# A block's 256 columns split into even and odd dims instead of two sets of samples, with an addition on VectorE before the sums over dims

## The reference

```
h = x
for i in 0, 1, 2:                       # W_i: (200, H_i * 40), H = 40, 100, 100
    p[b, h*40+m, d] = h[b, h, d] * x[b, m, d]
    y = relu(einsum('oi,bid->bod', W_i, p) + bias_i)
    h, direct_i = first and last 100 of y   # the last layer: all 200 are direct
z = concat(direct_0, direct_1, direct_2).sum over d      # (512, 400)
out = relu(relu([z, dense] @ W_top1 + b) @ W_top2 + b) @ W_top3
```

## Time and profile before

| | |
|---|---|
| median of 3 runs | 2904.6 us (2903.6 to 2905.39) |
| profiled execution | 2907.22 us, its span 2905.5 us |
| TensorE, matmuls busy | 2830.5 us, 97% of the span |
| VectorE busy | 2607.7 us, 90% |
| ScalarE busy | 1502.0 us, 52% |
| GpSimd busy | 688.1 us, 24% |

### The profile page before, as it was taken

How to read it: one execution, slowest core, us unless ns; L and a number is a source line. 1 busy time by engine, 2 the same in 40 slices (tenths; PEclk the granted TensorE clock), 3 DMA queues, 4 the chain that set the end, 5 groups by cost and what they waited for, 6 DMA issues and landing times.

```text
span 2905.5 us, 54782 instructions
## 1 busy us (share of the span) xinstructions
PE 2830.5 (97%) x19516; PEld 2811.0 (97%) x19516; DVE 2607.7 (90%) x1751; ACT 1502.0 (52%) x1880; POOL 688.1 (24%) x669
## 2 busy tenths in 40 slices
PE   2899999999999999999999999999999999999998
PEld 2899999999999999999999999999999999999996
DVE  4899999999999999999999999999999999999993
ACT  2555555555555555555555555555555555555552
POOL 2122222222222222222222222222222222222000
PEclk8999999999999999999999999999999999999999
DMA  6434333334333334333334334334333334334320
GB/s 158 101 67 100 86 74 97 86 74 98 87 74 96 87 74 99 87 74 97 87 75 98 86 74 97 87 75 96 89 73 96 88 75 99 87 75 94 95 57 21
DMA packets 280089, 249.92 MB, mean 86 GB/s; under 512 B 27803, under 2 KB 278602, under 8 KB 279965
## 3 DMA queue, kind: packets, MB, share of 16 engines
q1 hardware_dynamic: 211192, 196.57, 23.8%
q0 software_dynamic: 59744, 45.90, 11.0%
q10 hardware_dynamic: 9129, 7.13, 1.0%
HBM read 140.44 MB, written 4.20 MB: 50 GB/s over the span
## 4 chain that ended last, share of the span: by engine, by line
PE 96%; DMA 1%; SPq 1%; DVE 1%; issue 1%; ACT 0%; POOL 0%; DVEq 0%; ACTq 0%; POOLq 0%
PE acc L717 62%; PE acc L719 29%; PE z_ps L734 3%; PE hid_ps L730 1%; SPq L349 1%; PE acc L777 0%; DMA x_pairs<-x_rows 0%; DVE product L660 0%; DMA raw_weights<-in_w 0%; DVE tails L665 0%; PE hid_ps L800 0%; SPq L321 0%; DMA hid_rep<-hid 0%; POOL gathered L410 0%; DMA starts_sb<-in_table_starts 0%
## 5 line engine op out<-in xcount | busy, mean ns | idle before, releaser
L717 PE MATMUL acc<-weights,heads 126*128 126x400 f32 (+1 forms) x9088 | 2707.9, 365 | 62.3 <-DVE tails L665 62.3
L719 PE MATMUL acc<-weights,tails 126*128 126x200 f32 (+1 forms) x9088 | 2324.3, 256 | 0.0
L484 ACT ACTIVATE heads<-product 126x1024 fp32r<-126x1024 f32 (+2 forms) x1152 | 1203.9, 1048 | 1149.9 <-PE acc L719 749.5
L717 PEld LDWEIGHTS acc<-weights,heads 126*128 126x128 f32 (+1 forms) x9088 | 1717.0, 189 | 63.8 <-issue 46.6
L719 PEld LDWEIGHTS acc<-weights,tails 126*128 126x128 f32 (+1 forms) x9088 | 1744.7, 192 | 0.0
L660 DVE TENSOR_TENSOR product<-hid_rep,x_rep 126x2048 f32<-126x2048 f32 x512 | 1172.5, 2290 | 214.8 <-PE acc L719 175.5
L665 DVE TENSOR_TENSOR tails<-product,heads 126x1024 fp32r<-126x1024 f32 (+2 forms) x1152 | 1338.4, 1203 | 3.4 <-ACT heads L484 3.4
L418 POOL TENSOR_TENSOR wait_taker<-wait_taker 1x1 f32<-1x1 f32 x192 | 106.8, 556 | 2069.0 <-ACT acc_copy L490 2067.3
L410 POOL DMA_INDIRECT gathered<-in_table,rows_now x150 | 316.5, 2110 | 45.7 <-issue 45.7
L495 ACT ACTIVATE y_relu<-acc_copy 128x400 f32<-128x400 f32 x192 | 102.4, 533 | 192.8 <-DMA acc_copy<-acc_copy 192.8
L419 POOL DMA_DIRECT2D acc_copy<-acc_copy x192 | 175.8, 916 | 1.1 <-issue 0.6
(11 more groups left out here) (27 smaller groups left out, 106.4 us busy)
## 6 DMA issues: line engine op xcount, KB each, us to landing
x_rep<-x_rows SPq DMA_DIRECT2D x512, 120.0 KB
hid_rep<-hid SPq DMA_DIRECT2D x512, 120.0 KB
x_pairs<-x_rows SPq DMA_DIRECT2D x192, 280.0 KB
acc_copy<-acc_copy POOLq DMA_DIRECT2D x192, 200.0 KB
hid_rep<-hid SPq DMA_DIRECT2D x512, 5.0 KB
x_pairs<-x_rows SPq DMA_DIRECT2D x64, 120.0 KB
raw_weights<-in_w ACTq DMA_DIRECT2D x12, 492.2 KB
x_rep<-x_rows SPq DMA_DIRECT2D x128, 20.0 KB
```

What stands on the lines that cost most here:

```text
L484: act.activation(heads[0:rows, ring % HEADS_RING, 0:tiles, :], product[0:rows, ring % PRODUCT_RING, 0:tiles, :], ACT.Copy).then_inc(heads_ ...
L717: nc.tensor.matmul(acc[:, at.parity, c, 0:2 * LAYER], heads[0:rows, ring % HEADS_RING, k, cols], w, start=(q == 0 and k == 0), stop=False)
L719: last = nc.tensor.matmul(acc[:, at.parity, c, LAYER:2 * LAYER], tails[0:rows, ring % PRODUCT_RING, k, cols], w[:, 0:LAYER], start=False, ...
```

## The change

- `c` now means the parity of the dim, not the half of the samples: `dims(columns, c)` is `columns[:, c:256:2]`. The stationary operands of L717 and L719 are read with a step of two, and the transposes write `hid_ps` with a step of two, so that it has the columns in the old order. Row r of both result halves belongs to sample r // 16.
- VectorE gets a new instruction, `fold`: it adds the two halves of the direct outputs of `y_relu` into `y_fold`, 100 elements a partition for layers 0 and 1, 200 for layer 2. It waits for `y_relued` and for the turn before (`y_turned`).
- `turn` sums `y_fold` with `sum16` (128 x 8), one matmul for each 100 outputs in place of two, and waits for `y_folded` between the transposes and the sums.
- VectorE's order in the steady state: the fold of the step before's layer 2 lies between the tails of groups 2 and 3 of layer 1, the fold of layer 0 behind the tails of groups 4 and 5 of layer 1, the fold of layer 1 between the tails of groups 4 and 5 of layer 2.

```diff
+DIM_HALF = DIM // CG
...
+        y_fold = sb("y_fold", [128, LAYER])
...
-        sum32 = sb("sum32", [128, 128 // DIM])
+        sum16 = sb("sum16", [128, BLOCK])
...
+        def dims(columns, c):
+            return columns[:, c:COLS:CG]
...
+            def fold(layer, at, b):
+                first = HALF if layer < 2 else 0
+                dve.wait_ge(y_relued, at.slot + 1)
+                above_zero(dve, y_turned, at.slot)
+                dve.tensor_tensor(y_fold[:, first:LAYER], y_relu[:, 0, first:LAYER], y_relu[:, 1, first:LAYER],
+                                  ALU.add).then_inc(y_folded, 1)
+
-            def make_previous_tails(g, ring):
+            def make_previous_tails(g, ring, between=None):
                 layer, q = previous[0]
-                for n in (2, 1):
-                    make_tails(layer, q + 2 - n, g - n, (ring - n) % RING)
+                make_tails(layer, q, g - 2, (ring - 2) % RING)
+                if between:
+                    fold(*between)
+                make_tails(layer, q + 1, g - 1, (ring - 1) % RING)
                 previous[0] = None
...
+                        between = None
+                        if first and layer == first[0] and q == 4 and before and before[0] > 0:
+                            between = before
+                        if second and layer == second[0] and q == 6:
+                            between = first
                         if previous[0]:
-                            make_previous_tails(at.group + q, at.ring + q)
+                            make_previous_tails(at.group + q, at.ring + q, between)
+                            if l0 and first and layer == first[0] and q == 6:
+                                fold(*l0)
...
-                        cols = slice(c * 128, (c + 1) * 128)
-                        nc.tensor.matmul(acc[:, at.parity, c, 0:2 * LAYER], heads[0:rows, ring % HEADS_RING, k, cols], w,
+                        nc.tensor.matmul(acc[:, at.parity, c, 0:2 * LAYER], dims(heads[0:rows, ring % HEADS_RING, k, :], c), w,
                                          start=(q == 0 and k == 0), stop=False)
-                        last = nc.tensor.matmul(acc[:, at.parity, c, LAYER:2 * LAYER], tails[0:rows, ring % PRODUCT_RING, k, cols],
+                        last = nc.tensor.matmul(acc[:, at.parity, c, LAYER:2 * LAYER], dims(tails[0:rows, ring % PRODUCT_RING, k, :], c),
                                                 w[:, 0:LAYER], start=False, stop=(q == last_q and k == tiles - 1))
...
-                        nc.tensor.transpose(hid_ps[0:HALF, layer, c * 128:(c + 1) * 128], y_relu[:, c, 0:HALF], ident[:, :])
+                        nc.tensor.transpose(dims(hid_ps[0:HALF, layer, 0:COLS], c), y_relu[:, c, 0:HALF],
+                                            ident[:, :])
+                pe.wait_ge(y_folded, at.slot + 1)
                 for n, first in enumerate((HALF,) if layer < 2 else (0, HALF)):
-                    for c in range(CG):
-                        at_col = n * BLOCK + c * (BLOCK // CG)
-                        last = nc.tensor.matmul(z_ps[0:HALF, at.parity, at_col:at_col + BLOCK // CG],
-                                                y_relu[:, c, first:first + HALF], sum32[:, :], start=True, stop=True)
+                    last = nc.tensor.matmul(z_ps[0:HALF, at.parity, n * BLOCK:(n + 1) * BLOCK],
+                                            y_fold[:, first:first + HALF], sum16[:, :], start=True, stop=True)
```

More of the change, by code:

```diff
@@ L76, in cin_kernel @@
 def cin_kernel(nc, ids, table_starts, table, w0a, w0b, w1, w2, dense_t, wt1z, wt1d, wt2, wt3, bt1, bt2,
-               ident_in, sum32_in, out):
+               ident_in, sum16_in, out):
     duos = ids.shape[1]
@@ L190, in cin_kernel @@
         y_relued = sem("y_relued")
+        y_folded = sem("y_folded")
         y_turned = sem("y_turned")
@@ L312, in _ @@
                 sp.dma_start(swapped(n), w0b[:, t:t + k, :]).then_inc(swapped_loaded[n], 16)
-            for dst, src in ((ident[:, :], ident_in), (sum32[:, :], sum32_in), (dense_sb[:, :], dense_t),
+            for dst, src in ((ident[:, :], ident_in), (sum16[:, :], sum16_in), (dense_sb[:, :], dense_t),
                              (wt1d_sb[:, :], wt1d), (wt3_sb[:, :], wt3), (bt1_sb[:, :], bt1), (bt2_sb[:, :], bt2)):
@@ L670, in _ @@
             previous = [None]
-            def make_previous_tails(g, ring):
+            def fold(layer, at, b):
[5 more added lines that the diff above has]
+            def make_previous_tails(g, ring, between=None):
                 layer, q = previous[0]
-                for n in (2, 1):
-                    make_tails(layer, q + 2 - n, g - n, (ring - n) % RING)
+                make_tails(layer, q, g - 2, (ring - 2) % RING)
+                if between:
+                    fold(*between)
+                make_tails(layer, q + 1, g - 1, (ring - 1) % RING)
                 previous[0] = None
             def step(i, odd):
+                before, l0, l1, l2 = slots_of(i, odd)
+                first, second = (l1, l2) if l1 else (l2, None)
                 for layer in range(3):
@@ L692, in step @@
                             make_previous_tails(at.group + 2, at.ring + 2)
+                        if before and before[0] == 0 and layer == 0:
+                            fold(*before)
                         if odd is None:
@@ L698, in _ @@
             make_previous_tails(total_groups, total_groups)
+            fold(2, place(2, blocks - 1), blocks - 1)
         @block.tensor
@@ L845, in lay_out @@
     packed["ident"] = np.eye(128, dtype=np.float32)
-    packed["sum32"] = np.repeat(np.eye(128 // DIM, dtype=np.float32), DIM, axis=0)
+    packed["sum16"] = np.repeat(np.eye(BLOCK, dtype=np.float32), DIM_HALF, axis=0)
     tables = [arr(f"tbl_{f}") for f in range(FIELDS)]
@@ L863, in build @@
                args["w2"], args["dense_t"], args["wt1z"], args["wt1d"], args["wt2"], args["wt3"], args["bt1"],
-               args["bt2"], args["ident"], args["sum32"], out)
+               args["bt2"], args["ident"], args["sum16"], out)
 def kernel(**inputs):
```

## The result

| | median us | lowest to highest | runs |
|---|---|---|---|
| before | 2904.99 | 2903.6 to 2905.82 | 4 |
| after | 2937.35 | 2935.3 to 2939.8 | 4 |

The ratio is 1.0112, 95% interval [1.0095, 1.013]: 32 us slower, where 36 us faster was forecast. The profiled execution took 2935.3 us, its span 2933.6.

The account below looks back on a forecast made before the run. TensorE's instruction stream was taken to bound the kernel. -38 (z sums) + 2 (late folds) + 0 (stepped loads) + 0 (stepped PSUM writes) = -36, so 2869 us against the median of 2904.6; range 2857 to 2906.

Parts of the forecast that it names:

- What bounds the kernel: TensorE's instruction stream is the time: 142 pairs of heads and tails matmuls a block, 41.7 us, plus 1.85 us of turns.
- Part 1: TensorE's turns: 512 of 1024 z instructions go, 0.62 us a block, a gain of 38 us.
- Part 2: VectorE's three folds a block, 0.17, 0.17 and 0.27 us, mostly covered by slack: 2 us lost, bounds 0 and 21.
- covers: VectorE's 2.2 us of slack a block covers 0.61 us of folds; outside layer 1 TensorE needs them 0.3 us or more later.
- the tight place: Layer 1's fold behind its relu: z sums 0.15 to 0.2 us late in about one of five blocks, 0.03 a block.
- Part 3: Heads and tails stationary loads with a step of two cost 0; upper bound half rate, +820 to +1380 us.
- rival 1: The stepped stationary load is slower, in every pair's 0.09 us lead; 10% slower costs some 90 us, so 2959; chance 0.17.
- The lead: The 0.09 us from a heads load's start to its heads matmul, on the path in every pair; half rate adds 0.09.
- Stepped PSUM writes: The 256 transposes writing PSUM with a step of two cost 0; bounds 0 and 33 us, chance of slow writes 0.05.
- The range: 2857 to 2906 us for the whole kernel, leaving out the slower load and a little of the lower edge, 0.2.
- a pair at 0.30 or more: Sign of rival 1: heads matmul to heads matmul takes 0.30 us or more, where the forecast had 0.29.
- Loads over 0.19 in the mean: Sign of rival 1: stationary loads of heads and tails last over 0.19 us in the mean.

Follow-up runs that it names:

- no_step: The changed kernel with both stationary loads contiguous again, folds, four z sums and stepped transposes kept: 2868.7 us, ratio 0.9858 to the kernel before.
- step_only: The changed kernel without folds: loads stepped, each z sum as two accumulating matmuls over the halves: 2978.7 us, ratio 1.0242 to the kernel before.
- heads_step: The changed kernel with only the heads tiles read with a step, tails tiles contiguous: 2950.6 us, ratio 1.0145 to the kernel before.
- tails_step: The changed kernel with only the tails tiles read with a step, heads tiles contiguous: 2883.6 us, ratio 0.9914 to the kernel before.
- split_read: The changed kernel with both stationary loads contiguous; VectorE's product reads with a step of two and sorts even and odd columns: 2875.5 us, ratio 0.9889 to before.
- split_twice: split_read run again, unchanged, on the same chip as split_inc: 2880.5 us, ratio 0.9912 to the kernel before.
- split_inc: split_read with GpSimd taking its wait by a semaphore instruction in place of the 1-element addition: 2870.4 us, ratio 0.9864 to the kernel before.
- step4: The changed kernel with stationary columns taken with a step of four over two neighbouring tiles: 4421.6 us, ratio 1.5216 to the kernel before.

## Why the prediction was wrong

- *What bounds the kernel*: right. The pair's time times 9088, with 38 us off for the turns where there are folds, gives `no_step`, `step_only`, `heads_step` and `tails_step` within 5 us.
- *Part 1, fewer z sums, -38 us*: right. `no_step` is 38 us faster than before with it, folds included (36 forecast for both).
- *Part 2, folds, +2 us*: the prices 0.17 and 0.27 us were measured at 0.17 and 0.28, their covers held, TensorE waited 0.2 us for them from 150 to 2800 us of the kernel after. The slack of 0.2 us behind layer 1's relu was seen as the tight place, but only with relus as late as in the kernel before. Where TensorE does get faster, VectorE gets denser, and then GpSimd's addition takes up to 6.8 us. The prediction had neither that path nor the fall of TensorE's clock behind a stall. In `split_read` the two are worth about 10 us (`split_twice` less `split_inc`), not 2; in `no_step` they show as a spread of 13 us about the forecast 2869.
- *Part 3, stepped load, 0*: this is the step that failed. It was mis-sized: 7 ns a load and 7.8 ns a pair, where the bounds went from 0 to 150 and the gain would have been eaten by 4.0. The place was right (rival 1: the load is on the path in each pair). The argument for zero was a comparison of rates: 9.5 bytes a ns wanted, 8 shown by the moving operand's reads. That row covers 8 (8.6 if the tails matmul is taken alone, 200 columns in 92.6 ns), not 9.5, and I waved the rest through. The measured limit of a load is 8.8 to 9.3. Read properly, the row said "nothing above 8.6 is shown", and with the gain eaten at 4% of a load this asked for a chance nearer a half than 0.17. Rival 1's price was nearly sound: at 9 to 11 ns a pair for a load 10% longer, one 6.4% longer makes 6 to 7, where 7.8 were measured. At about half rate, in `step4`, a pair costs 171 ns more (4422 less 2869, over 9088), where the bound was 150.
- *The lead*: I put the cost in the 0.09 us from heads load to heads matmul. That interval did not grow (the heads load starts with the tails matmul before it, and from that matmul to the next heads matmul it is 92.7 and 92.1 ns); it is the tails load's start that moves. `heads_step` and `tails_step` show it.
- *Stepped PSUM writes, 0*: right for these 256 transposes, 0.22 us for two before and after, and all of them are in `no_step`. The Trainium skill's "PSUM — Partial Sum Buffer" ("Specifications (TRN2)") warns of them; no loss shows here. That they stay hidden behind the load is argued, not shown.
- *The range* ended at 2906 because it left the slower load out as a whole, with its 0.17. 2937 lies where rival 1 was expected (above 2911).
- *The signs*: "a pair at 0.30 or more" came as said (0.303). "Loads over 0.19 in the mean" told little: the kernel before had 0.189 and 0.192 already.

## What to carry to other kernels

Before an operand of a saturated engine gets a step, price it at the number of times it is read: here 512 instructions saved at 75 ns were outweighed by 9088 pairs made 8 ns longer. A rate that a row shows covers what is at or below it, not a fifth above. If an order of columns is wanted, let an engine with slack write it (VectorE's stepped reads were free) and keep the stationary operand contiguous. And look at what a fuller VectorE delays on GpSimd: a stall of TensorE is paid twice, once as the wait and once in its clock.

## What the runs showed of the hardware

- A load of 128 fp32r stationary columns takes 108.7 ns to the next load when contiguous, 115.7, 165.1 and 233.5 at steps of two, three and four: from two on 1.7 to 1.8 ns for each 16 bytes swept.
- Of the two loads of a pair, a step in the first costs 82 us over 9088 pairs and in the second 15, and in both together 69 to 71, less than in the first alone.
- A GpSimd addition of a single element took up to 6.76 us beside a VectorE that issued two-input instructions back to back, and ended within 52 ns of the end of a VectorE instruction (all 76 that took over 2 us). With a semaphore instruction in its place the longest waits of the relu fell from 6.8 to 4.2 us.
- Behind a stall of TensorE of 3.73 us its granted clock was 0.53 for 7 us, and it did 23 matmuls in them instead of 49.
- Reads with a step of two fp32 on both inputs cost VectorE nothing: 2021 ns for a product of 1792 elements, 2025 without the step.
